# Two small matmuls become VectorE adds: layer 2's second bias, and layer 1's residual row with bc

## The reference, cut to what matters

```
# layer 1, "attention": a linear recurrence over the 256 tokens of a row
x_b   = xn @ Wb.T + bb
h_all = scan over t:  h[t] = lam * h[t-1] + (1 - lam) * x_b[t]
z     = (h_all @ Wc.T + bc) + xn
z     = (z - mean(z)) / sqrt(var(z) + 1e-5) * gamma + beta     # x += z

# layer 2, feed-forward: 8 experts, each token goes to its best one
h1 = relu(xn @ W1[e] + b1[e]);  ye = h1 @ W2[e] + b2[e]        # x += gate * ye
```

## Time and profile before

| what | value |
|---|---|
| time, median of 3 runs (lowest, highest) | 1804.51 us (1802.91, 1811.77) |
| span of the profiled execution, first to last instruction | 1781.4 us |
| median of the runs less that span | 23.1 us |
| PE busy, DVE busy, ACT busy, POOL busy | 85%, 64%, 49%, 25% of the span |
| mean granted TensorE clock | 0.903 of 2.4 GHz |
| layer 1's turns, from about 655 to 930 us | 16 turns, 16.7 us each |
| layer 2's turns with blocks, from about 1035 to 1347 us | 13 turns, about 24.1 us each |

### The profile page before, as it was taken

One profiled execution on the slowest core, in us unless ns is written; L12 is line 12 of the kernel. 1 busy time (PEld: TensorE's weight loads), 2 busy tenths in 40 slices (PEclk: granted clock), 3 DMA queues, 4 the chain that ended last, 5 costly groups with the idle time before them and its releaser, 6 DMA issues.

```text
span 1781.4 us, 41543 instructions
## 1 busy us (share of the span) xinstructions
PE 1516.1 (85%) x11849; PEld 962.0 (54%) x11849; DVE 1140.7 (64%) x3250; ACT 866.4 (49%) x1971; POOL 443.6 (25%) x542
## 2 busy tenths in 40 slices
PE   5457999998989769999986688898999698999997
PEld 4123666665655258888875245555554255555554
DVE  6734666666667755656556556566668567777774
ACT  1023444454445324444431255556565177788887
POOL 3475332322322202222223712212213100000000
PEclk9567999998999659999995689999999689999999
DMA  8442454454444113333220324333342011111110
GB/s 257 131 156 65 137 168 145 141 172 124 143 136 136 26 54 137 113 124 142 107 83 26 113 79 131 123 105 121 109 127 76 30 44 51 47 51 49 47 52 11
DMA packets 127956, 182.18 MB, mean 102 GB/s; under 512 B 14824, under 2 KB 107296, under 8 KB 125424
## 3 DMA queue, kind: packets, MB, share of 16 engines
q1 hardware_dynamic: 94944, 141.94, 24.7%
q10 hardware_dynamic: 26112, 25.17, 4.8%
q0 software_dynamic: 6816, 14.02, 2.2%
HBM read 145.84 MB, written 42.84 MB: 106 GB/s over the span
## 4 chain that ended last, share of the span: by engine, by line
PE 62%; DVE 16%; issue 8%; ACT 4%; POOL 4%; DMA 4%; DVEq 1%; SPq 0%; ACTq 0%; POOLq 0%
PE pO L739 8%; PE pH L530 7%; PE pH L622 7%; PE pY L543 6%; PE pT_ L596 6%; PE pY L630 6%; DVE mx L1343 4%; PE pS L682 3%; PE pS L704 3%; POOL sorted_x L995 2%; ACT pex L853 2%; PE pT_ L594 2%; PE pT_ L514 2%; DVE ob L1421 1%; PE pS L506 1%
## 5 line engine op out<-in xcount | busy, mean ns | idle before, releaser
L853 ACT ACTIVATE pex<-pT_ 128x512 f32<-128x512 f32 (+1 forms) x768 | 427.0, 560 | 481.1 <-PE pT_ L596 367.2
L1343 DVE TENSOR_REDUCE mx<-pS 128x2 f32<-128x512 f32 x512 | 346.9, 689 | 137.0 <-PE pS L573 122.5
L596 PE MATMUL pT_<-stk 32*128 32x256 f16 x1024 | 199.0, 283 | 71.5 <-DVE mx L1343 29.3
L894 POOL DMA_INDIRECT home_y<-ysb,home x117 | 115.1, 984 | 547.9 <-DVE ysb L1365 348.4
L573 PE MATMUL pS<-stk 32*128 32x256 f16 x1024 | 207.0, 289 | 22.6 <-DVEq L1086 17.6
L739 PE MATMUL pO<-pex,va 128*9 128x256 f32 (+1 forms) x3072 | 204.7, 387 | 2.7 <-ACT pex L853 2.7
L846 ACT ACTIVATE wb<-pH,b 128x256 f32<-128x256 f32 x256 | 107.3, 470 | 113.3 <-PE pH L530 112.9
L596 PEld LDWEIGHTS pT_<-stk 32*128 32x128 f16 x1024 | 55.0, 93 | 183.8 <-issue 87.6
L530 PE MATMUL pH<-XT,w 128*128 (+1 forms) x512 | 131.9, 385 | 1.1
L622 PE MATMUL pH<-xsT,wb 128*128 128x128 f32 x888 | 132.5, 294 | 0.3 <-ACT xsT L822 0.3
L630 PE MATMUL pY<-wb,hbs 128*128 128x128 f32 x888 | 128.5, 288 | 3.0 <-DVE ysb L1365 3.0
(11 more groups left out here) (222 smaller groups left out, 2626.8 us busy)
## 6 DMA issues: line engine op xcount, KB each, us to landing
wb<-in_w SPq DMA_DIRECT2D x111, 514.0 KB, 4.9
stk<-packed_qk ACTq DMA_DIRECT2D x96, 256.0 KB, 2.7
packed_qk<-qk SPq DMA_DIRECT2D x144, 128.0 KB, 2.1
wb<-gates_turned SPq DMA_DIRECT2D x8, 2048.0 KB, 7.0
pex<-gates_turned SPq DMA_DIRECT2D x8, 2048.0 KB, 7.0
xsb<-sorted_x SPq DMA_DIRECT2D x111, 64.5 KB, 2.1
sorted_x<-in_c_places SPq DMA_DIRECT2D x4, 1548.0 KB, 16.1
XN<-home_y SPq DMA_DIRECT2D x16, 256.0 KB, 5.1
```

What stands on the lines that cost most here:

```text
L596: return pe.matmul(bank[:, part * T:(part + 1) * T], key, stk[rows, side, j, 0:T], start=True, stop=True)
L853: ins = act.activation(pex[:, k % 8, 0:n], bank[:, 0:n], ACT.Exp)
L894: pool.indirect_dma_start(YH, bass.IndirectOffsetOnAxis(ap=home[:, place_:place_ + 1], axis=0), ysb[:, place_, :], None).then_inc(sem(f"ho ...
L1343: ins = dve.tensor_reduce(mx[:, :, j, col], bank.rearrange("p (c n) -> p c n", c=2), AX.X, ALU.max)
```

## The change

In layer 1, step Z, the two identity matmuls go. PE no longer waits for `row_staged`. POOL now makes `xtb` from XN (tokens on partitions) and `bc1`, which is now loaded to all partitions as a row of 128. DVE waits for `row_staged`, adds bank and `xtb` into `zn`, waits for that, and frees the bank there; statistics and normalization read `zn` in place of the bank. In layer 2 the fifth matmul of Y goes, and the copy of `ysb` becomes an add of the block's `b2`, which is now 128 further columns of the block's weights, the same on every partition (4624 bytes a partition in place of 4112). The tile `wb2`, its DMA and the tile of ones `onesr` go.

```diff
-        wb = sb("wb", [P, RING_IN, WROW])
-        wb2 = sb("wb2", [1, RING_IN, P])
+        wb = sb("wb", [P, RING_IN, WROW + P])
...
-        bc1 = sb("bc1", [P, 1])
+        bc1 = sb("bc1", [P, P])
...
 PE, Y of layers 0 and 2
-                                            stop=(f == NF - 1 and l == 0))
-                        if l == 2:
-                            ins = pe.matmul(pY[:, 0:P], onesr[:, :], wb2[:, place_, :], start=False, stop=True)
+                                            stop=(f == NF - 1))
...
 PE, Z
-                        pe.wait_ge(s("row_staged"), PRIMED + turn.row(1))
                         for c in range(2):
-                            o = bank[:, c * P:(c + 1) * P]
-                            pe.matmul(o, hT[:, c * P:(c + 1) * P], wc1[:, :], start=True, stop=False)
-                            ins = pe.matmul(o, xtb[:, par, c * P:(c + 1) * P], ident[:, :], start=False, stop=True)
+                            ins = pe.matmul(bank[:, c * P:(c + 1) * P], hT[:, c * P:(c + 1) * P], wc1[:, :],
+                                            start=True, stop=True)
...
 POOL, stage of layer 1
-                        pool.tensor_tensor(xtb[:, par, :], XT[:, bass.ts(turn.row(1), T)],
-                                           bc1[:, 0:1].to_broadcast([P, T]), ALU.add).then_inc(s("row_staged"), 1)
+                        pool.tensor_tensor(xtb[:, par, :].rearrange("p (c n) -> p c n", c=2),
+                                           XN[:, bass.ds(turn.count(2, 2), 2), 0:P],
+                                           bc1[:, None, :].to_broadcast([P, 2, P]), ALU.add)\
+                            .then_inc(s("row_staged"), 1)
...
 DVE, Y of layers 0 and 2
-                        dve.tensor_copy(ysb[:, place_, :], yb[:, 0:P]).then_inc(s("Y_free"), 1)
+                        if l == 0:
+                            ins = dve.tensor_copy(ysb[:, place_, :], yb[:, 0:P])
+                        else:
+                            ins = dve.tensor_tensor(ysb[:, place_, :], yb[:, 0:P], wb[:, place_, WROW:WROW + P], ALU.add)
+                        ins.then_inc(s("Y_free"), 1)
...
 DVE, Z and N
-                        z_bank = bank
+                        dve.wait_ge(s("row_staged"), PRIMED + turn.row(1))
+                        settle(dve, sem("dve_settled"))
+                        tc.link(dve.tensor_tensor(zn[:, :, :], both(bank[:, 0:2 * P]), both(xtb[:, par, :]), ALU.add))
+                        dve.sem_inc(s("S_free"), 1)
                         for c in range(2):
-                            m = tc.mark(dve.bn_stats(zs[:, c, :], z_bank[:, c * P:(c + 1) * P]))
+                            m = tc.mark(dve.bn_stats(zs[:, c, :], zn[:, c, :]))
...
-                            m = tc.mark(dve.tensor_scalar(zn[:, c, :], z_bank[:, c * P:(c + 1) * P],
+                            m = tc.mark(dve.tensor_scalar(zn[:, c, :], zn[:, c, :],
                                                           zmv[:, c, 0:1], zr[:, c:c + 1], ALU.subtract, ALU.mult))
                         tc.wait(m)
-                        dve.sem_inc(s("S_free"), 1)
...
 SP, load_weights
-                sp.dma_start(wb[:, ring, :], d[f"w_{l}"][bass.ds(e, 1), :, :].rearrange("e p n -> (e p) n"))\
+                sp.dma_start(wb[:, ring, 0:WROW + (P if l == 2 else 0)],
+                             d[f"w_{l}"][bass.ds(e, 1), :, :].rearrange("e p n -> (e p) n"))\
                   .then_inc(sem(f"w_in{ring}"), 16)
-                if l == 2:
-                    sp.dma_start(wb2[:, ring, :], d["b2_2"][bass.ds(e, 1), :]).then_inc(sem(f"w_in{ring}"), 16)
...
 host layout
+    b2 = np.broadcast_to(a["L2_ffn_b2"][:, None, :], (8, P, P))
+    o["w_2"] = np.concatenate([a["L2_ffn_W1"], w2(a["L2_ffn_W2"]), b1, b2], axis=2)
```

More of the change, by code:

```diff
@@ L356, in build @@
         ident = sb("ident", [P, P])
-        onesr = sb("onesr", [1, P])
         onesm = sb("onesm", [P, P])
@@ L431, in build @@
                      (bv0[:, :], d["bv0"].partition_broadcast(P))],
-            "ld_cst": [(onesr[:, :], d["c_ones"][0:1, :]), (onesm[:, :], d["c_ones"]),
+            "ld_cst": [(onesm[:, :], d["c_ones"]),
                        (maskb[:, :, :], d["c_mask"]), (identb[:, :], d["c_identb"]), (later[:, :], d["c_later"]), (rank[:, :, :], d["c_rank"]),
@@ L438, in build @@
                      (b2[1][:, :], d["b2_1"]), (wb1[:, :], d["wb1"]), (wc1[:, :], d["wc1"]), (bb1[:, :], d["bb1"]),
-                     (bc1[:, :], d["bc1"]), (gam1[:, :], d["gam1"].partition_broadcast(P)),
+                     (bc1[:, :], d["bc1"].partition_broadcast(P)), (gam1[:, :], d["gam1"].partition_broadcast(P)),
                      (bet1[:, :], d["bet1"].partition_broadcast(P)), (llr1[:, :], d["llr1"])],
@@ L479, in expert_in @@
         def expert_in(turn, rounds):
-            return rounds * 16 if turn.layer == 0 else rounds * 32 + 16 * before_in
+            return rounds * 16 + (0 if turn.layer == 0 else 16 * before_in)
         def homes_in(l):
@@ L1654, in lay_out @@
     o["wb1"], o["wc1"] = a["L1_attn_Wb"].T, a["L1_attn_Wc"].T
-    o["bb1"], o["bc1"] = a["L1_attn_bb"].reshape(P, 1), a["L1_attn_bc"].reshape(P, 1)
+    o["bb1"], o["bc1"] = a["L1_attn_bb"].reshape(P, 1), a["L1_attn_bc"]
     o["gam1"], o["bet1"] = a["L1_attn_gamma"], a["L1_attn_beta"]
@@ L1660, in lay_out @@
     b1 = a["L2_ffn_b1"].reshape(8, NF, P).transpose(0, 2, 1)
-    o["w_2"] = np.concatenate([a["L2_ffn_W1"], w2(a["L2_ffn_W2"]), b1], axis=2)
-    o["b2_2"] = a["L2_ffn_b2"]
+    b2 = np.broadcast_to(a["L2_ffn_b2"][:, None, :], (8, P, P))
+    o["w_2"] = np.concatenate([a["L2_ffn_W1"], w2(a["L2_ffn_W2"]), b1, b2], axis=2)
     o["wq3"] = a["L3_attn_W_attn"].reshape(P, 3, P)
```

## The result

On the chip of the recorded runs the changed kernel took 1792.22 us (median of 5, 1783.31 to 1796.15) and the kernel before 1804.24 us (median of 5). The ratio is 0.9913, with an interval of 0.989 to 0.9935: 15.7 us off (11.7 to 19.8). The two medians lie 12.0 us apart; where this text says how much was gained, it goes by the ratio, which has the interval. The forecast was 1783, with a range of 1777 to 1793. So it is faster, and by less than the 21.2 us of the sum. All ratios leave out four executions, one each of e1, e2, e8 and the kernel before, that ran 4% to 93% longer.

The account below looks back on a forecast made before the run. PE's matmuls were taken to bound most of the kernel, alternating with DVE in layer 2. 6.6 + 15.0 - 0.4 = 21.2 us off took 1804.5 to 1783.3, stated as 1783, range 1777 to 1793.

Parts of the forecast that it names:

- the sum: Whole kernel: 6.6 us from layer 1 plus 15.0 from layer 2 minus 0.4 for the add, 21.2 us off.
- Rival B: Layer 2: the `stk` load becomes the bound, 0.82 us lost in twelve turns, 9.8 us, time 1793; chance 0.10.
- rival E: Layer 2: the removed matmul L634 is cheap, 0.22 us each, 8 us in all, time 1790; chance 0.07.
- Layer 1 off PE, 6.6 us: Layer 1, step Z: two identity matmuls removed save 0.44 us a turn over 15 turns, 6.6 us.
- DVE's 0.72 a turn: Layer 1: the new add, 0.415 us, plus a 0.31 us wait, hidden by DVE's idle time.
- Layer 2's fifth matmul, 0.41 each: Layer 2, Y: removing the matmul with b2 saves 0.41 us a block, 1.23 us a turn of three blocks.
- The lower bound, 0.22: Layer 2: the removed matmul priced like layer 1's cheapest two-record matmul, 0.22 us, 8 us in all.
- The sum over the turns, 15.0: Layer 2: 39 blocks give 16.0 us, one turn loses 0.82, leaving 15.2; with the chain's 14.1, taken as 15.0.
- What is late next: Layer 2: PE reaches S1 0.82 us earlier and waits 0.3 us for `stk`, hidden, with some 0.3 us room.
- the late turn: Layer 2: one turn whose chain runs through POOL, stores and `stk` load; only 0.41 us gained, 0.82 lost.
- Weights wider, 0: Layer 2: weights grow by an eighth but stay three blocks ahead, a whole turn, costing 0.
- The median as span plus 23.1: Whole kernel: the runs' median is 23.1 us over the profiled span, so span 1760 becomes 1783.3.

Follow-up runs that it names:

- e1: Kernel before with only the change's layer 1 lines, layer 2 as before; median 1775.46 us, ratio to the kernel before 0.9978.
- e2: Kernel before with only the change's layer 2 lines, layer 1 as before; median 1775.91 us, ratio to the kernel before 0.9966.
- e8: Changed kernel with two more 128x256 DVE maximum operations in each turn of layer 1; 1800.4 us, ratio to the kernel before 0.9964.
- e3: The changed kernel run again unaltered in another session; median 1765.82 us, ratio to the kernel before 0.9894.
- e4: The kernel before, unaltered, timed against itself and profiled a second time; median 1781.54 us, ratio 1.001.
- e5: Changed kernel with POOL making both halves of layer 2's split ahead of sending Y0 home; 1792.73 us, ratio to the kernel before 0.9928.
- e6: Changed kernel without layer 2's second bias: plain copy, weights of 4112 bytes a partition; 1791.28 us, ratio to the kernel before 0.9915.
- e7: Kernel before, all matmuls kept, with layer 2's wide weights load whose last 128 columns nobody reads; 1804.45 us, ratio to the kernel before 0.9994.
- e10: Changed kernel with 24 empty instructions on DVE ahead of layer 2; median 1786.27 us, ratio to the kernel before 0.9888.
- e11: Changed kernel with 48 empty instructions on DVE ahead of layer 2; median 1797.39 us, ratio to the kernel before 0.9943.
- e12: Changed kernel with 24 empty instructions on PE ahead of layer 2, none on DVE; median 1782.42 us, ratio to the kernel before 0.9866.

## Why the prediction was right and wrong

**The forecast as a whole.** Its direction was right, and 1792.22 lies inside 1777 to 1793, by 0.8 us. The range reached up to 1793 for rivals B and E, neither of which came as it stood, so that the time is inside owes something to luck.

**Layer 1 off PE, 6.6 us: right.** The stage is 6.8 us shorter in the recorded run, and 6.6 (e1) and 5.6 (e3) against e4. DVE's 0.72 a turn, measured 0.77, was hidden, as forecast; the cover was larger than read, 0.65 us behind it by e8.

**Layer 2's fifth matmul, 0.41 each: right for a turn.** 1.29 us a turn for three, 0.43 each. The 0.06 us a turn beyond the forecast can lie in V0's first two records, which the next T follows 0.32 us after their start in place of 0.42. The lower bound, 0.22, is out, and with it rival E. The one-row matmul was not as cheap as its neighbours. By the Trainium skill ("TensorE: Matmul & The Clock Gate", "Part 2: What happens when you issue a matmul"), a weight load's time does not depend on the row count. For the load itself the trace agrees: 182 ns for the one-row load (L634), 191 for those of 128 rows (L630). What the prediction drew from it for the whole matmul, 3 x 0.27 = 0.81 us a turn, did not come; the runs say 1.29. Where in the matmul the rest lies is open.

**The sum over the turns, 15.0: mis-sized.** Layer 2 gained 6.9 us in the recorded run (11.6 in e2, 10.0 in e3). The step that failed is "What is late next". It saw that PE would wait 0.3 us for the `stk` load in an ordinary turn and that this would stay hidden, and so it was; but it asked about the ordinary turn only. It did not ask what stands next to it on SP's queue. The change brings the weights load of the middle block nearer to the `stk` load, from 2.2 to 1.5 us behind it, 0.5 by the shorter turn and 0.2 by SP's own shorter list. Where a turn is disturbed enough (a load of instructions in turn 1, POOL's late start in turn 4), that is too little, the weights' packets go first, the landing takes 4.4 to 4.7 us, and PE's pause is followed by the lower clock. Rival B had the right place and the wrong number of turns: not a steady 0.82 in twelve turns, but about 5 us in one turn or two of the first four. These should have gained 5.2 us; in the recorded run they lost 3.9, so the shortfall is 9.1, in e3 it is 6.1 and in e2 4.6. The prediction let the late turn gain 0.41 of its 1.23; in all but e5 it grew, by 1.2 to 2.8.

**Weights wider, 0: right** (e6, e7). **One DMA fewer, 0: not shown**; it lets SP issue the weights 0.2 us sooner, which counts in turn 4. **The add, 0.4: right**, 281 ns.

**Ahead of layer 2's first send, 0: wrong by 3 us.** 121.5 us and more in every kernel with a changed layer 2, against 118.8. e7, which keeps the matmuls, has 123.4, and e6, which keeps the narrow load, 122.6. What it is remains open. In e10 and e11 it is 124.2 and 126.4, the empty instructions on DVE's way among it. The lower clock held for 88.7 us of this stretch in before, e1 and e4, for 92.2 or 95.6 in the others and for 102.4 in e10 and e11; whether that is the cause or only goes with it, no run shows.

**The median as span plus 23.1: wrong.** It is span plus 1.9; the profile of before is some 21 us shorter than its timed runs. By the spread of the runs (1783.3 to 1796.2 after) a single span says nothing within 10 us. The forecast was built on a difference from the median, so that this did no harm to it. From the terms as measured, 6.8 + 6.9 - 3.0 = 10.7 us off in the recorded execution; the ratio says 15.7 (11.7 to 19.8), of which the rest of the program, whose stretches differ by several us from one execution to the next, is not attributed.

Still open: whose instructions the first 16 KB load brings, how much of turn 1 and of turn 4 would have been lost with the old matmuls or with the DMA of `b2` kept, and the 3 us. A version in which SP issues the middle block's weights only behind the `stk` load was not run; by e5's turn 4 (21.13 against some 26.5) it would be worth up to 5 us there, an estimate. Of those run, e12 has the lowest ratio, 0.9866 (0.9825 to 0.9907), but its interval overlaps that of the changed kernel, so it is not shown to be faster.

## What to carry to other kernels

When a stage gets shorter, list the transfers whose distance to each other goes by its length, and not only the engine waits: a load that has 1.5 us to its neighbour on another queue is safe in the steady turn and lost in the first disturbed one. Look at the unrolled turns and the first pass of a loop apart from the steady ones; here four turns of thirteen took back 4.6 to 9.1 of some 16 us in the recorded run, e3 and e2, and 2.6 to 9.7 over all ten profiles. And before a small effect is put down to the edit, move the code by a few empty instructions and see whether it stays: 24 on PE (0.9866, 0.9825 to 0.9907) and 48 on DVE (0.9943, 0.9916 to 0.9969) lie 0.8% apart.

## What the runs showed of the hardware

- A 16 KB packet of the instruction queue took 0.9 to 1.7 us of a DMA engine's time in layer 2's first turns, and up to 2.5 us elsewhere. Beside one of 0.95 us, three rows of a weights load were done 1.8 us after the other 125, and the dependent load was issued 2 us late.
- Two loads on different queues, issued within about half a microsecond, did not share the engines evenly: the 256 KB load took 2.3 to 2.9 us where its packets started first and 4.4 to 4.7 us where the 578 KB load's did (and the same behind a 514 KB one, e6).
- A fifth matmul with one row in the contraction cost 0.43 us, a full 128-row one of the same width 0.27, although its weight load took 182 ns against 191.
- Behind pauses of PE of 1.24 and 1.32 us in the same turn of two kernels with the same matmuls, the granted clock fell to 1.2 GHz for 3.4 us in one and stayed at 2.4 GHz in the other: 24.60 and 23.13 us.
